# An eight-layer kernel on one core: the tail of the Mamba layer, its router and half of the last routing move inside the scan, and the last expert layer runs as two passes over halves of the tokens

## The reference, cut to what matters

```python
# layer 6: Mamba. D_INNER = 256 channels, D_STATE = 16
x_act = silu(conv(x @ in_proj_w.T ...));  delta = softplus(x_act @ dt_proj_w.T + b)
B_p, C_p = split(x_act @ x_proj_w.T)            # 16 values of each for every token
def step(h, inp):
    dA = exp(d_i[..., None] * A)
    h = dA * h + (d_i * u_i)[..., None] * B_i[:, None, :]
    y = einsum('bdn,bn->bd', h, C_i)
y = (ys + x_act * D_param) * silu(z);  return y @ out_proj_w.T
# layer 7: 16 experts of width 64, 4 groups of which the best 2 stay, top 4 experts, one shared expert
scores = sigmoid(xf @ gate_w.T);  s = scores + gate_bias
group_scores = s.reshape(T, 4, 4).max(-1);  keep = the 2 best groups;  idx = top_k(s where kept, 4)
comb = scores at idx, else 0
y = einsum('tei,edi,te->td', silu(x w1) * (x w3), w2, comb)
z = silu(x ws1) * (x ws3) @ ws2;  return y + z
```

## Time and profile before

| | |
|---|---|
| median of 3 runs | 1141.77 us |
| the profiled execution, time / span | 1142.86 us / 1141.0 us |
| TensorE matmul busy | 948.3 us, 83% |
| VectorE busy | 832.1 us, 73% |
| ScalarE busy | 654.1 us, 57% |
| GpSimd busy | 647.2 us, 57% |
| mean granted clock of TensorE | 0.936 |

### The profile page before, as it was taken

How to read it: one execution, slowest core, us unless ns; L and a number is a source line. 1 busy time by engine, 2 the same in 40 slices (tenths; PEclk the granted TensorE clock), 3 DMA queues, 4 the chain that set the end, 5 groups by cost and what they waited for, 6 DMA issues and landing times.

```text
span 1141.0 us, 11497 instructions
## 1 busy us (share of the span) xinstructions
PE 948.3 (83%) x2997; PEld 551.8 (48%) x2997; DVE 832.1 (73%) x1167; ACT 654.1 (57%) x1192; POOL 647.2 (57%) x454
## 2 busy tenths in 40 slices
PE   6879985788899867999999999875877777874996
PEld 3324332233357544788888887321323232343884
DVE  5995348999955587666666666688999999544664
ACT  5756666201366653565555565877766666272555
POOL 3030135698831224677777777106999999342772
PEclk9979998799999958999999999985999999987999
DMA  2000110000020003767676664000000000003651
GB/s 79 1 0 1 62 60 17 0 0 1 0 69 1 15 23 98 161 154 152 137 159 141 152 153 109 2 1 0 0 1 0 1 0 0 15 7 77 140 125 37
DMA packets 19367, 61.32 MB, mean 54 GB/s; under 512 B 2704, under 2 KB 12560, under 8 KB 14096
## 3 DMA queue, kind: packets, MB, share of 16 engines
q1 hardware_dynamic: 19328, 60.87, 22.5%
HBM read 59.15 MB, written 1.70 MB: 53 GB/s over the span
## 4 chain that ended last, share of the span: by engine, by line
PE 34%; POOL 10%; DVE 8%; issue 6%; ACT 2%; DMA 1%; POOLq 0%; SPq 0%; DVEq 0%; ACTq 0%
PE ps L520 33%; POOL g L2042 7%; DVE y L2770 2%; DVE g L2726 1%; DVE tmp L2070 1%; POOL tmp L2051 1%; POOL rstd L2051 1%; DVE resid L2070 1%; ACT g L1217 1%; DVE g L2770 1%; DMA g<-coef_scratch 1%; ACT rstd L1217 1%; DVE g L2070 0%; POOL parts L1891 0%; DVE rstd L2070 0%
## 5 line engine op out<-in xcount | busy, mean ns | idle before, releaser
L520 PE MATMUL ps<-parts 128*128 128x512 f32 x1704 | 418.4, 405 | 24.1 <-DVE g L2070 9.0
L520 PEld LDWEIGHTS ps<-parts 128*128 128x128 f32 x1704 | 324.4, 191 | 113.5 <-issue 17.7
L1217 ACT ACTIVATE g<-ps 128x512 f32<-128x512 f32 (+2 forms) x289 | 170.2, 594 | 181.9 <-PE ps L520 162.4
L1947 POOL TENSOR_TENSOR parts<-g,parts 128x512 fp32r<-128x512 f32 x148 | 191.2, 1292 | 105.4 <-ACT parts L1217 101.8
L520 PE MATMUL ps<-g,arena 128*128 128x512 f32 (+2 forms) x408 | 194.5, 618 | 34.9 <-POOL g L2003 15.1
L2070 DVE TENSOR_TENSOR ps<-g,ps 128x512 f32<-128x512 f32 x160 | 111.3, 696 | 102.1 <-PE ps L520 82.5
L2042 POOL TENSOR_TENSOR g<-g 128x1024 f32<-128x1024 f32 x64 | 149.2, 2362 | 52.4 <-DVE g L2070 52.0
L520 PEld LDWEIGHTS ps<-g,arena 128*128 128x128 f32 (+1 forms) x408 | 77.5, 199 | 143.8 <-issue 88.2
L1217 ACT ACTIVATE parts<-g 128x512 fp32r<-128x512 f32 (+2 forms) x252 | 126.5, 533 | 26.3 <-DVE g L2070 18.6
L2070 DVE TENSOR_TENSOR g<-ps,g 128x512 f32<-128x512 f32 (+1 forms) x164 | 115.6, 705 | 31.1 <-DMA g<-coef_scratch 9.3
L1217 ACT ACTIVATE ps<-g,small 128x512 f32<-128x512 f32 x131 | 85.2, 682 | 51.9 <-DVE g L2770 29.7
(11 more groups left out here) (202 smaller groups left out, 1149.7 us busy)
## 6 DMA issues: line engine op xcount, KB each, us to landing
g<-coef_scratch SPq DMA_DIRECT2D x72, 512.0 KB, 6.2
g<-in_moe_dram SPq DMA_DIRECT2D x42, 192.0 KB, 4.7
g<-coef_scratch SPq DMA_DIRECT2D x16, 256.0 KB, 5.7
g<-in_rope_dram SPq DMA_DIRECT2D x1, 2048.0 KB, 8.5
arena<-in_weights_dram SPq DMA_DIRECT2D x1, 1348.5 KB, 5.7
arena<-in_weights_dram SPq DMA_DIRECT2D x1, 1028.5 KB, 4.8
g<-in_x_dram SPq DMA_DIRECT2D x4, 256.0 KB, 4.0
out_dram<-g SPq DMA_DIRECT2D x4, 256.0 KB, 2.5
```

The source lines that it names most:

```text
L520: return nc.tensor.matmul(o, lhsT, rhs, start=start, stop=stop, **kw)
L1217: return nc.scalar.activation(o, i, func, **kw)
L1947: pv.tensor_tensor(hid_lo[:, cols(c)], g[:, 6, (c % 2) * N:(c % 2 + 1) * N], hid_hi[:, cols(c)].bitcast(F32), ALU.subtract).then_inc(s["hl ...
```

## The change

- **In the scan**: B is no longer spread by TensorE and copied by ScalarE. ScalarE copies the 16 rows of B of each chunk to SBUF (`b_copied`), SyncE stores them in DRAM (`b_scratch`), and each step's row is read back by one DMA that spreads it over 128 partitions (256 KB, four buffers, each refilled once GpSimd has used it). The decays take three PSUM banks in turn in place of four, and `hs_done` counts each half of a scan.
- **The tail of layer 6 for chunks 0 to 2** stands inside the scan of the next chunk: `out_of`, `post6_square`, `post6_var`, `post6_root`, `add_back6`, `pre7_square`, `pre7_var`, `pre7_root`, `h_back7`, `router7`, `clip7`. Squares of the second norm go from GpSimd to ScalarE. Only chunk 3 is left for behind the scan.
- **The routing** is done in halves of 8 tiles. The one for chunks 0 and 1 stands in VectorE's stream at steps 53, 54, 55 and 57 of the scan, the one for chunks 2 and 3 between the first `glu7`s. The sigmoid is made of Exp, Ln and Exp.
- **Layer 7** runs as 36 unrolled turns in the order `TURNS7`: rounds 0 to 8 for chunks 0 and 1, then rounds 0 to 8 for chunks 2 and 3. All nine pairs of weights are loaded and split ahead and stay in SBUF. Coefficients come as halves of a row.
- **The end**: post-norm of chunks 0 and 1 starts within the second pass (`y_copy`, `centre7`, `post7_square`). GpSimd adds `resid` to `mean0` there (`ends_added`), so that one addition a chunk on VectorE goes.

```diff
+TURNS7 = [(r, c) for half in ((0, 1), (2, 3)) for r in range(9) for c in half]
-DA_BANKS = (2, 6)
+DA_BANKS = (2, 3, 6)
 # SyncE
+                    for step in range(STEPS):
+                        k = step % 4
+                        if step < 4:
+                            sp.wait_ge(s["dl_ready"], step + 1)
+                        else:
+                            sp.wait_ge(s["db_ready"], step - 3)
+                        if step == 0:
+                            sp.wait_ge(s["b_stored"], 16 * CHUNKS)
+                        sp.dma_start(b_copy(step), b_dram[step % 16:step % 16 + 1, cols(step // 16)].to_broadcast([P, N]))\
+                          .then_inc(s[f"row_loaded{k}"], 16)
 # TensorE
-            def spread_b(step):
-                at_least(pe, s["bs_ready"], step)
-                mm(ps[:, B_BANK, :], row(step % 16), bc_rows[:, cols(step // 16)]).then_inc(s["bb_bank"], 1)
             for step in range(STEPS + 3):
-                if step + 4 < STEPS:
-                    spread_b(step + 4)
+                c, n = step // 16 - 1, step % 16
                 if step >= 3:
                     sum_n(step - 3)
+                if c >= 0 and step < STEPS:
+                    if n == 3:
+                        out_of(c)
+                    if n == 6:
+                        post6_var(c)
+                    if n == (10, 10, 13)[c]:
+                        pre7_var(c)
+                    if n == (13, 13, 15)[c]:
+                        router7(c)
+            gate_up7(0)
+            out_of(3)
+            gate_up7(1)
+            post6_var(3)
+            pre7_var(3)
+            router7(3)
+            for n in range(2, len(TURNS7)):
+                gate_up7(n)
+                if n >= 3:
+                    down7(n - 3)
+                if n == 14:
+                    coef_turned7(2)
+                    coef_turned7(3)
 # ScalarE, behind the scan
-            def copy_b(step):
+            input7_hi(2)
+            post6_square(3)
+            post6_root(3)
+            pre7_square(3)
+            pre7_root(3)
+            sigmoid7(1)
+            for n in range(len(TURNS7)):
+                silu(n)
 # VectorE, in the scan
             scan(0)
-            for step in range(STEPS):
-                if step % 16 == 3 and step > 3:
-                    gate(step // 16 - 1)
+            for k in range(STEPS):
+                c, n = k // 16 - 1, k % 16
+                if c >= 0:
+                    if n == 3:
+                        gate(c)
+                    if n == 8:
+                        add_back6(c)
+                    if n == (12, 12, 14)[c]:
+                        h_back7(c)
+                    if n == (14, 14, 15)[c]:
+                        clip7(c)
+                if k == 53:
+                    group_scores7(0)
+                if k == 54:
+                    group_order7(0)
+                if k == 55:
+                    kept7(0)
+                if k == 57:
+                    chosen7(0)
+                if k + 1 < STEPS:
+                    scan(k + 1)
```

More of the change, by code:

```diff
@@ new lines, in sigmoid7, with coef_copied7 @@
+            def sigmoid7(half):
+                both = score7[:, half * 128:(half + 1) * 128]
+                act.wait_ge(s["sc_clipped"], 2 * half + 4)
+                chain(f(both, both, ACT.Exp, scale=-1.0))
+                chain.wait()
+                chain(f(both, both, ACT.Ln, bias=one))
+                chain.wait()
+                f(both, both, ACT.Exp, scale=-1.0).then_inc(s["sc_copied"], 1)
+            def coef_copied7(c):
+                bank = {0: variance7(0), 1: centred7(1), 2: ps[:, 2, :], 3: ps[:, 3, :]}[c]
+                act.wait_ge(s["ct_bank"], CHUNKS + c + 1)
+                f(coef_rows7[:, cols(c)], bank[0:16, :], ACT.Copy).then_inc(s["ct_ready"], 1)
@@ new lines, in kept7 @@
+            def kept7(half):
+                biased, better, ahead, best7, keep7, top7, padded, out_padded = scratch7(half)
+                step(v.tensor_reduce(keep7, by(better, GROUPS), AX_X, ALU.add))
+                step(v.tensor_scalar(keep7, keep7, float(KEEP), 2 * BIG, ALU.is_lt, ALU.mult))
+                step(v.scalar_tensor_tensor(
+                    padded[:, :, 0:E].rearrange("p a (q e) -> p a q e", e=E // GROUPS),
+                    by(keep7, GROUPS).unsqueeze(3).to_broadcast([P, A7, GROUPS, E // GROUPS]), -BIG,
+                    biased.rearrange("p (a q e) -> p a q e", q=GROUPS, e=E // GROUPS), ALU.add, ALU.min))
+                for a in range(A7):
+                    last = v.max(top7[:, a, :], padded[:, a, 0:E])
+                step(last)
```

770 lines of the change are left out of this document (499 added, 271 removed).

## The result

The changed kernel takes 1132.19 us in the median of six runs (1129.56 to 1137.0). The kernel before took 1142.07 us beside it (1140.77 to 1143.28, six runs). The ratio is 0.9927 with a 95% interval of 0.991 to 0.9945, so it is faster by 9.9 us. The forecast was 13.8 us and 1128.0 us. The result lies in the range on record, 1117 to 1139, and just above the band of 1124 to 1132 that had the largest chance. The execution profiled took 1132.16 us.

What follows compares the result with a forecast made beforehand. VectorE was taken to bound the scan, chains between engines the tail and first rounds, TensorE the later rounds. +21.7 - 10.9 - 18.8 - 5.8 = -13.8 us gave 1128.0 us for the median, range 1117 to 1139.

Steps and rivals of the forecast that it cites:

- The bound of the scan, and B: Scan: VectorE sets its pace, so taking B from TensorE and ScalarE gains nothing; reads of B stay hidden, 0.
- Entry, +3.0: Scan's start: ScalarE's copies of B, last store and first read delay the first product by 3.0 us (bounds 0 and 5).
- VectorE's new work, +6.3 and +4.9: Scan: three instructions and a clip for each of chunks 0 to 2 add 6.3 us, routing of half 0 adds 4.9.
- The port, +6.5: Scan: eight routing instructions contend with GpSimd and wait, 6.5 us (bounds 0 and 18.9).
- the two rivals on the port: Port waits cost nothing, 1119.5 us (chance 0.17), or all they can, 18.9 in the scan, 1140.4 us (0.16).
- Their waits are covered: Scan: VectorE's new layernorm instructions wait for nothing, as ScalarE's Ln and Exp stand four steps ahead of their reader.
- the +1.0: Behind the last scan: chunk 2's router among TensorE's four sums delays the last gate by 1.0 us.
- Gate to running rounds, -10.9: Last gate to running rounds: one chunk in place of four takes 17.0 us in place of 27.9, gain 10.9.
- The rounds, -18.8: Layer 7's rounds: first half's coefficients ready before the first turn, 78.8 us in place of 97.6, gain 18.8.
- The end, -5.8: Behind the last turn: squares of chunks 0 and 1 already done, 18.0 us in place of 23.8, gain 5.8.
- The rival of the clock: Scan: with fewer spreads TensorE falls to half clock, each cold step costs 0.9 us, forty give 1164 us; chance 0.08.
- The sum: Whole kernel: +21.7 to the last gate, -10.9, -18.8 and -5.8 behind it, in all -13.8 us.

Runs made afterwards that it cites:

- b_alone: The kernel before, with only B changed to come by DMA in place of TensorE's spread and ScalarE's copy; 1144.15 us, ratio 1.0012.
- a_both: The changed kernel with chunk 2's tail put later and the first half's routing moved behind the last gate; 1115.55 us, ratio 0.976.
- a_later: The changed kernel with two pieces of the first half's routing one step later, at 55 and 56; 1126.61 us, ratio 0.9868.
- a_tail: The changed kernel with h_back7(2), router7(2) and clip7(2) put later, the clip behind the last gate; 1128.43 us, ratio 0.9873.
- a_move: The changed kernel with the first half's routing moved from the scan to behind the last gate, nothing left out; 1121.78 us, ratio 0.9815.
- a_busy: The changed kernel with zero-matrix multiplications added on TensorE, 26 at step 54 and 14 at step 57; 1130.61 us, ratio 0.9897.
- a_pieces: a_both with the second half's routing cut into seven pieces in place of three; 1114.1 us, ratio 0.9736.

## Why the prediction was right, and where it was off

**The bound of the scan, and B.** Right. Taking 64 matmuls from TensorE and 64 copies from ScalarE changed the scan by nothing (b_alone, 209.9 us both). But TensorE did not fall to the 58% busy of the prediction: it is 138.36 of 202.50 us there, 68%, partly because its matmuls take longer at the low clock. The reads landed in 3.3 us, sooner than the 5.7 taken from the coefficients, and GpSimd never waited for one.

**Entry, +3.0.** The traces have +2.8, but this point wanders by 7 us with the clock of the layers ahead, so the agreement proves little.

**VectorE's new work, +6.3 and +4.9.** The layernorm's instructions came to 6.1 us, the half's routing with GpSimd idle to 5.1 (0.61 + 1.18 + 1.57 + 1.73 in `a_both`).

**The port, +6.5.** 5.8, shown by moving the same instructions away from GpSimd. The mechanism is shown by the single durations and by `a_later`: for the four chained ones I had waits of 0.8 + 2.4 + 2.4, and the trace has 0.7 + 2.1 + 2.0. The prediction also has it that an instruction with at most one SBUF input does not contend with GpSimd. `a_later` has one that waited, the `tensor_scalar` of 1.08 us; the `times_c` of a PSUM and an SBUF input took 1.2 us beside GpSimd throughout. Of the two rivals on the port neither came true.

**"Their waits are covered": the step that failed.** The prediction put the waits of VectorE's new instructions at nothing, since ScalarE's Ln and Exp stand four steps earlier than their reader. That is wrong for every chunk. In chunks 0 and 1 `pre7_root` and its reader `h_back7` both stand at step 12 of their scan; in chunk 0 the Exp ended at 876.81 and the reader began at 876.84, so it was covered with nothing to spare. For chunk 2 `pre7_var` stands at step 61 and `pre7_root` at 63, `router7` at 63, and VectorE reads at 62 and 63. The root stands behind its reader, and the two readers stand ahead of `scan(63)` and of the last `times_c`. In place of nothing VectorE waited 2.04 us for ScalarE and 3.00 for TensorE's router.

The account of the +26.9: entry 2.8, layernorm 6.1, routing with its port waits 10.9, VectorE idle up to the end of the last scan 6.1 (2.04 and 0.31 for ScalarE, 1.89 for TensorE's C, 1.3 ahead of the two other clips, the rest small), and 0.9 more from there to the gate; I had 3.0, 6.3, 11.4, 0 and 1.0. So the mis-sized term is the waiting, 0 in place of 6.1; the other four came 0.1 to 0.5 lower each, which leaves about the 5.2. The 3.00 us of the router are not in the 6.1: they lie in the last stretch, which grew by only 0.9 because the wait for the sums behind it shrank from 5.65 to 3.90. That the +1.0 came out there is luck, since it was counted as work of TensorE's router. Of the 6.1, the 1.89 and 0.31 follow the low clock from 988 to 996, not the order of the tail. What the order of chunk 2's tail costs in all shows only when it is taken away: 4.5 us in `a_tail`, 7.0 in `a_both`, of which 3.35 are the low clock that `a_move` has there.

**Gate to running rounds, -10.9.** Measured -10.2: 17.6 us against 17.0. **The rounds, -18.8.** Measured -21.1. The mechanism was right (coefficients of the first half ready before the first turn, no gap); the additions to the 70.1 us of matmuls were mis-sized, 6.7 in place of 8.7. The slow start cost 2.1 us in place of 3.0 (the first 54 took 14.63, at 0.2315 each they would take 12.5), transposes and means 2.1 in place of 2.7, and the second half's routing made TensorE wait 1.27 + 0.64 = 1.9 us, 2.5 forecast; its coefficients were asked for 7.1 us before they were wanted (issued at 1072.86, wanted at 1079.98). **The end, -5.8.** Measured -6.4, of which the early post-norm is only 2.6.

**The rival of the clock.** It came in part. The clock fell to 0.50 between 972 and 980, where VectorE was held by the port for 6 us and TensorE had no work, and to 0.53 to 0.90 in a few windows besides. In the profile of the changed kernel it cost about 2 us, the waits of 1.89 and 0.31; `a_later`, whose clock was up again in time, is without both. `a_busy` took the first away and paid 1.7 us later. The sentence that a backlog fills the engine and so brings the clock back is borne out: from 848 on each fall in the profile of the changed kernel was over within 4 to 16 us. The Trainium skill, "TensorE: Matmul & The Clock Gate", section "HAM oscillation — how this bites in real kernels", has a kernel falling back again and again. That is nearer to what the scan now does than my chance of 0.08 allowed; but the cold steps were a few, not forty, and most cost nothing.

**The sum.** -10.9 in the traces against -13.8: +5.2 in the scan, +0.7 in the chain, -2.3 and -0.6 in rounds and end.

## What to carry to other kernels

When work of an earlier chunk is woven into a loop, write down for each chunk how many steps lie between each producer and its reader. The last chunk is the one whose tail is squeezed against the loop's end, and there a reader ahead of the loop's last instructions holds up everything. Put small instructions with two SBUF inputs where GpSimd is idle: behind the last gate the same routing cost nothing, in the scan 10 us, of which 5.8 were port waits. And when two waits cover one another (a cold clock and a long piece on another engine), an experiment that removes one shows little: remove both. When a low clock goes from one place, look where else it has come up before you call it free.

## What the runs showed of the hardware that was not expected

- TensorE's clock fell in the scan at nearly the same places in several kernels (windows near 848, 868 and 904 us, at 0.5 to 0.9), also in the kernel before with B taken off TensorE alone (near 848, 900 and 952), and not at all between 800 and 972 in the kernel before. In the profile of `a_pieces` TensorE had waited 2.33 us ahead of 922.59, and the windows from 920 to 928 show 0.82 and 0.75.
- Programs that differ ahead of the scan by four copies reach it between 779.7 and 787.1 us, by the clock that was granted until then (0.95 to 0.93). Differences of a few us between single profiles mean nothing unless they are counted from an event behind that.
- A `tensor_scalar` of 128x32 with a single SBUF input took 1.08 us beside GpSimd and 0.18 without: it waits as those with two inputs do.
